# Fetching the shifted rows of v inside SBUF instead of through DRAM, with the middle row read in place

## What is computed

```python
def _dcn(x, ...):
    xproj = x @ inproj_w + inproj_b                      # v: the values that are sampled
    x1 = gelu(layernorm(dwconv3x3(x)))
    offset = x1 @ off_w + off_b
    m = softmax((x1 @ mask_w + mask_b).reshape(B, H, W, G, P), -1)
    out = _dcnv3_core(xproj, offset, m)                  # sampling, 8 groups x 9 points
    return out @ outproj_w + outproj_b

def _dcnv3_core(x, offset, mask):
    xp = pad(x, 1)
    loc = ref + dil_grid + offset / norm                 # 9 points per group and pixel
    # bilinear: 4 neighbours of each point, each weighted, zero outside the padded image
    sampled = gather(y0, x0) * w00 + gather(y0, x1) * w01 + gather(y1, x0) * w10 + gather(y1, x1) * w11
    return (sampled * m).sum(-1)
```

## Time and profile before

| | us |
|---|---|
| median of 3 runs | 101.66 |
| the profiled execution | 101.21 |
| its span (first to last instruction) | 99.3 |
| PE, DVE, ACT, POOL busy | 87.2, 60.1, 45.5, 31.7 |

### The profile page before, as it was taken

How to read it: one execution, slowest core, us unless ns; L and a number is a source line. 1 busy time by engine, 2 the same in 40 slices (tenths; PEclk the granted TensorE clock), 3 DMA queues, 4 the chain that set the end, 5 groups by cost and what they waited for, 6 DMA issues and landing times.

```text
span 99.3 us, 2669 instructions
## 1 busy us (share of the span) xinstructions
PE 87.2 (88%) x1109; PEld 58.3 (59%) x1109; DVE 60.1 (61%) x149; ACT 45.5 (46%) x100; POOL 31.7 (32%) x47
## 2 busy tenths in 40 slices
PE   4989999999978999119999999898999997799980
PEld 1446568558948998013473476574977785564330
DVE  1269673215899929579603416697830969827770
ACT  0470076479887110100003344869535889785000
POOL 7979988500034729779200000000000000400000
PEclk9999999999999999955599999999999999999999
DMA  1996000000448999600000000000000000000003
GB/s 27 367 424 241 23 0 7 0 7 0 160 103 219 219 239 201 139 0 7 3 7 0 0 7 0 0 0 0 0 0 7 0 0 0 0 0 0 0 7 109
DMA packets 1869, 6.26 MB, mean 63 GB/s; under 512 B 288, under 2 KB 800, under 8 KB 1600
## 3 DMA queue, kind: packets, MB, share of 16 engines
q1 hardware_dynamic: 1424, 4.66, 17.9%
q10 hardware_dynamic: 432, 1.42, 3.7%
HBM read 5.16 MB, written 0.92 MB: 61 GB/s over the span
## 4 chain that ended last, share of the span: by engine, by line
PE 56%; DMA 16%; DVE 13%; ACT 6%; SPq 2%; issue 2%; DVEq 0%; ACTq 0%
PE ps L1193 55%; DMA v_win<-v_padded 13%; DMA v_padded<-v_tok 3%; ACT prod L804 2%; SPq L521 2%; DVE prod L984 2%; ACT prod L867 1%; DVE smax L1025 1%; DVE prod L1059 1%; ACT upad L702 1%; DVE res L1188 1%; DVE prod L1063 1%; DVE v_tok L922 1%; DVE ln_room L975 1%; SPq L514 1%
## 5 line engine op out<-in xcount | busy, mean ns | idle before, releaser
L1193 PE MATMUL ps<-terms,wts 64*128 64x256 f32 (+4 forms) x72 | 12.5, 365 | 1.8 <-DVE terms L958 0.9
L1193 PE MATMUL ps<-prod,ident 32*32 32x512 f32 (+1 forms) x216 | 10.3, 755 | 3.7 <-DVE prod L984 3.7
L688 POOL TENSOR_TENSOR terms<-terms 128x256 f32<-128x256 f32 x2 | 1.5, 750 | 36.3 <-DVE terms L1075 36.3
L1193 PEld LDWEIGHTS ps<-terms,wts 128*128 128x128 f32 (+1 forms) x72 | 9.1, 189 | 3.8 <-issue 1.4
L1193 PE MATMUL ps<-prod,wts 128*64 128x256 f32 (+1 forms) x56 | 10.8, 394 | 0.2
L984 DVE TENSOR_TENSOR prod<-v_win,ps 128x1280 f32<-128x1280 f32 x6 | 8.6, 1481 | 3.6 <-DMA v_win<-v_padded 3.6
L603 POOL TENSOR_TENSOR prod<-v_win,a_rows_sb 128x1280 f32<-128x1280 f32 x4 | 9.6, 2413 | 3.1 <-DMA v_win<-v_padded 3.1
L1193 PEld LDWEIGHTS ps<-prod,ident 32*32 32x32 f32 (+1 forms) x216 | 5.2, 118 | 7.6 <-issue 6.4
L1193 PEld LDWEIGHTS ps<-prod,wts 128*64 128x64 f32 (+1 forms) x56 | 6.0, 158 | 3.6 <-DVE prod L1183 1.3
L611 POOL TENSOR_TENSOR terms<-ym,near_hat 128x864 f32<-128x864 f32 x2 | 4.0, 2024 | 12.1 <-DVE ym L950 12.1
L1193 PE MATMUL ps<-idle 128*128 128x512 bf16 x19 | 6.6, 486 | 1.3 <-DVE idle L873 1.3
(11 more groups left out here) (182 smaller groups left out, 172.2 us busy)
## 6 DMA issues: line engine op xcount, KB each, us to landing
v_win<-v_padded SPq DMA_DIRECT2D x4, 640.0 KB, 9.2
wts<-in_w ACTq DMA_DIRECT2D x1, 984.0 KB, 8.1
wts<-in_w SPq DMA_DIRECT2D x1, 640.0 KB, 7.7
v_padded<-v_tok SPq DMA_DIRECT2D x4, 128.0 KB, 3.0
wts<-in_w ACTq DMA_DIRECT2D x1, 280.0 KB, 4.1
x_in<-in_x SPq DMA_DIRECT2D x1, 256.0 KB, 3.2
out<-res SPq DMA_DIRECT2D x2, 128.0 KB, 1.9
wts<-in_w SPq DMA_DIRECT2D x1, 193.0 KB, 3.9
```

Source lines behind the costliest of these rows:

```text
L688: g.tensor_tensor(base_out[:, bl, :], t2[:, bl, :], x2[:, bl, :], ALU.add).then_inc(base_done, 1)
L1193: return nc.tensor.matmul(out_, lhsT, rhs, start=start, stop=stop, skip_group_check=True)
```

## The change

It replaces the way through DRAM by transfers from v_tok to v_win inside SBUF. For dy = 3, 0, 4, 1 and each half of partitions one transfer shifts v_tok by 4 or 8 partitions into the row dy of v_win (60 or 56 partitions of 2 KB), eight per bl, sixteen in all. The edge partitions of each row, for which the window lies outside the image, are cleared ahead by eight small transfers into v_win. The row dy = 2 isn't copied: `window(bl, 2)` reads v_tok itself. VectorE does the rows in the order 2, 0, 1 and waits for v_above[bl] (rows 0 and 1) only at the rows 0 and 1; GpSimd waits for v_below[bl] (rows 3 and 4). TensorE sums in the order 2, 3, 0, 1, 4. The image in DRAM is still stored, behind the row transfers, for the far branch, which now waits for v_stored.

```diff
--- before.py
+++ after.py
@@ -42,7 +42,7 @@
 
 VP = math.isqrt(XQ * VR * VWX - 1) + 1
 
-ROWS = (0, 1, 3, 2, 4)
+ROWS = (2, 3, 0, 1, 4)
 TILE = 32
 TG = P // TILE
 PE5, PE3 = 20, 9
@@ -52,7 +52,11 @@
 
 POOLED = (3, 4)
 
-PRODUCT_ORDER = ((0, 0), (0, 1), (0, 2), (1, 0), (1, 1), (1, 2))
+
+VECTOR_ROWS = (2, 0, 1)
+PRODUCT_ORDER = tuple((bl, dy) for bl in range(BL) for dy in VECTOR_ROWS)
+
+FETCHED = (3, 0, 4, 1)
 
 WARM = {"projection": 8, "conv5": 2, "weights": 3, "close_l0": 2, "route": 4}
 
@@ -129,7 +133,7 @@
         sq, lnv, rstd, xn = (ln_room[:, i * BL:(i + 1) * BL, :] for i in range(4))
         x1 = sb("x1", [P, BL, HW])
         v_tok = sb("v_tok", [P, BL, CELLS])
-        v_win = sb("v_win", [P, BL, K5, VWX * C])
+        v_win = sb("v_win", [P, BL, K5, CELLS])
         past = sb("past", [P, BL, 2 * NPT * XG])
         minus_ident = sb("minus_ident", [P, P])
         lmax = sb("lmax", [P, BL, XG])
@@ -166,7 +170,7 @@
         s_min = sb("s_min", [P, NPT * XG])
         s_v = sb("s_v", [P, W * C])
 
-        zeros = s_v[0:B * XQ, 0:2 * CELLS]
+        zeros = s_v[0:2 * XQ, 0:BL * CELLS]
 
         v_blocks = v_dram.rearrange("b y x c -> b (y x c)")[:, 0:XQ * VR * CELLS].rearrange(
             "b (q r n) -> b q r n", q=XQ, r=VR)
@@ -256,7 +260,7 @@
         x_loaded = sem("x_loaded")
         pads_zero = sem("pads_zero")
         zeros_set = sem("zeros_set")
-        v_cleared = sem("v_cleared")
+        edges_cleared = sem("edges_cleared")
         ones_set = sem("ones_set")
         idle_set = sem("idle_set")
         diag5_set = sem("diag5_set")
@@ -385,13 +389,31 @@
 
         route_step = [sem(f"route_step{bl}") for bl in range(BL)]
         v_stored = [sem(f"v_stored{bl}") for bl in range(BL)]
-        v_windowed = [sem(f"v_windowed{bl}") for bl in range(BL)]
+        v_above = [sem(f"v_above{bl}") for bl in range(BL)]
+        v_below = [sem(f"v_below{bl}") for bl in range(BL)]
         slow_loaded = [sem(f"slow_loaded{bl}") for bl in range(BL)]
 
 
         def grid(ap):
 
             return ap.rearrange("p (y x) -> p y x", y=H)
+
+        def edge_rows(bh, dy):
+
+            p0, p1_ = half(bh)
+            n = abs(dy - K5 // 2) * XQ
+            return (p0, p0 + n) if dy < K5 // 2 else (p1_ - n, p1_)
+
+        def inner_rows(bh, dy):
+
+            p0, p1_ = half(bh)
+            n = abs(dy - K5 // 2) * XQ
+            return (p0 + n, p1_) if dy < K5 // 2 else (p0, p1_ - n)
+
+        def window(bl, dy):
+
+            row = v_tok[:, bl, 0:VW] if dy == K5 // 2 else v_win[:, bl, dy, 0:VW]
+            return bass.AP(row.tensor, row.offset, [list(row.ap[0]), [C, K5], [GC, XG], [1, GC]])
 
         def tokens(tile, bl, bh, xl):
 
@@ -501,25 +523,27 @@
                 sp.dma_start(wts[:, CUTS[i]:CUTS[i + 1]], A_w[:, CUTS[i]:CUTS[i + 1]]).then_inc(w_loaded[i], 16)
 
             sp.wait_ge(zeros_set, 1)
-            for r in (0, VR - 2):
-                for b in range(B):
-                    sp.dma_start(v_blocks[b, :, r:r + 2, :].rearrange("q r n -> q (r n)"),
-                                 zeros[b * XQ:(b + 1) * XQ, :]).then_inc(v_cleared, 16)
-            sp.wait_ge(v_cleared, 2 * B * 16)
+            for dy in FETCHED:
+                for bh in range(BH):
+                    e0, e1 = edge_rows(bh, dy)
+                    sp.dma_start(v_win[e0:e1, :, dy, :], zeros[0:e1 - e0, :].rearrange("p (b n) -> p b n", b=BL)
+                                 ).then_inc(edges_cleared, 16)
+            sp.wait_ge(edges_cleared, len(FETCHED) * BH * 16)
             for bl in range(BL):
                 sp.wait_ge(v_copied, bl + 1)
+                for dy in FETCHED:
+                    for bh in range(BH):
+                        d0, d1_ = inner_rows(bh, dy)
+                        s0 = d0 + (dy - K5 // 2) * XQ
+                        sp.dma_start(v_win[d0:d1_, bl, dy, :], v_tok[s0:s0 + d1_ - d0, bl, :]).then_inc(
+                            (v_above if dy < K5 // 2 else v_below)[bl], 16)
+            for bl in range(BL):
                 for bh in range(BH):
                     p0, p1_ = half(bh)
                     inside = v_blocks[BL * bh + bl, :, 2:2 + H, :].rearrange("q y n -> y q n")
                     sp.dma_start(inside, v_tok[p0:p1_, bl, :]).then_inc(v_stored[bl], 16)
             for bl in range(BL):
                 sp.wait_ge(v_stored[bl], 16 * BH)
-                for bh in range(BH):
-                    p0, p1_ = half(bh)
-                    rows = bass.AP(v_dram.tensor, v_blocks[BL * bh + bl, 0, 0].offset,
-                                   [[CELLS, H], [VR * CELLS, XQ], [1, K5 * CELLS]])
-                    sp.dma_start(v_win[p0:p1_, bl, :, :].rearrange("p y n -> p (y n)"),
-                                 rows).then_inc(v_windowed[bl], 16)
             for bl in range(BL):
                 sp.wait_ge(res_done, bl + 1)
                 sp.dma_start(out[:, bl * HW:(bl + 1) * HW], res[:, bl, :]).then_inc(out_stored, 16)
@@ -595,10 +619,9 @@
 
             def products(bl, dy):
 
-                pool.wait_ge(v_windowed[bl], 16 * BH)
+                pool.wait_ge(v_below[bl], 16 * BH * len(POOLED))
                 pool.wait_ge(a5_copied, bl + 1)
-                row = v_win[:, bl, dy, 0:VW]
-                win = bass.AP(row.tensor, row.offset, [list(row.ap[0]), [C, K5], [GC, XG], [1, GC]])
+                win = window(bl, dy)
                 weights = a5_rows_sb[:, bl, dy - AR, :].rearrange("p (d x) -> p d x", d=K5)
                 g.tensor_tensor(prod[:, bl, dy, :, :].rearrange("p d (x c) -> p d x c", c=GC), win,
                                 weights.unsqueeze(3).broadcast_to([P, K5, XG, GC]),
@@ -623,6 +646,7 @@
                 with pool.If(is_far > 0):
 
                     pool.wait_ge(samp_done, bl + 1)
+                    pool.wait_ge(v_stored[bl], 16 * BH)
 
                     pos = s_pos[:, bl, :, :].rearrange("p c n -> p (c n)")
                     for axis in range(2):
@@ -976,11 +1000,12 @@
 
             def products(bl, dy):
 
-                if dy == 0:
-                    dve.wait_ge(v_windowed[bl], 16 * BH)
+                if dy == K5 // 2:
+                    dve.wait_ge(v_copied, bl + 1)
                     dve.wait_ge(a5_done, bl + 1)
-                row = v_win[:, bl, dy, 0:VW]
-                win = bass.AP(row.tensor, row.offset, [list(row.ap[0]), [C, K5], [GC, XG], [1, GC]])
+                else:
+                    dve.wait_ge(v_above[bl], 16 * BH * (K5 // 2))
+                win = window(bl, dy)
                 v.tensor_tensor(prod[:, bl, dy, :, :].rearrange("p d (x c) -> p d x c", c=GC), win,
                                 a5_rows(bl, dy, dy + 1)[:, 0].unsqueeze(3).broadcast_to([P, K5, XG, GC]),
                                 ALU.mult).then_inc(prod_done, 1)
@@ -1084,9 +1109,9 @@
             far_terms(1, 0)
             far_terms(1, 2)
             for bl in range(BL):
-                for dy in range(K5 - len(POOLED)):
+                for dy in VECTOR_ROWS:
                     products(bl, dy)
-                    if bl and dy == 1:
+                    if bl and dy == VECTOR_ROWS[0]:
                         flags(0)
                         flags(1)
             mask_sums(0)
```

## The result

The changed kernel takes 96.56 us (median of 4 runs, 96.16 to 96.85), the kernel before beside it 101.69 us. The ratio is 0.952, 95% interval 0.946 to 0.957. On another chip, with more runs, it was 0.943 (0.938 to 0.948). The prediction was 96.3, with a range of 95.2 to 98.5.

A forecast was written before the change was run, and what follows sets the result against it. It took the v passage through DRAM, mostly volume, and the slab sum's halved clock as the bound. An earlier start (2.9 us) and full clock (2.2) gave 5.1 us: 96.1 from the profile, 96.6 from the median, stated 96.3, range 95.2 to 98.5.

The forecast's parts named there:

- The floor: Start of half 1's products: gate moves from the 42.73 set by DRAM to about 39.80, set by a5_done(1).
- The slab sum: TensorE's window sum: starts 41.43, takes 7.1 us at full clock, ends 48.5 instead of 53.61; gain 5.1 us.
- B: Rival: TensorE's clock falls all the same, slab sum keeps 9.25 us; gain 2.9, 98.3 us; chance 0.10.
- GpSimd: GpSimd's products of rows 3 and 4: half 1's end at 42.76 and 45.15, neither later than TensorE.
- The transfers: 16 SBUF-to-SBUF transfers on SP's queue: 0.64 us an issue, some 4 us of margin everywhere, cost 0.
- The landing: Time from a row transfer's issue to its landing: taken as 3.3 us, from a span of 1.9 to 3.3.
- the 38 that was to show it right: Sign for the row transfers into v_win: all 16 landed before 38 us.
- Rival C: SBUF-to-SBUF transfers move at half rate, 108 GB/s, 1.1 us each; gain 3.7, 97.5 us; chance 0.08.
- Rival D: Row transfers become the wait: at 1.24 us each, 102.9 us; decides from 1.13 us a transfer; chance 0.03.
- Rival E: Each row transfer pays its landing before the next begins: 16 take 30.4 us, time 110.3 us; chance 0.01.
- The clears: Eight edge clears, now into SBUF: at 4.6 to 7.1 us as before, with time until 24 us.
- VectorE: VectorE's six products as before: 1.48 us each, 1.43 apart, three in 4.28 us.

The follow-up runs named there:

- e1: The kernel before, with 14 dummy matmuls put into TensorE's wait ahead of the slab sum; ratio 0.964 (0.957 to 0.970).
- e3: The kernel before, five rows still loaded from DRAM, middle row multiplied in place and first, sum order 2, 3, 0, 1, 4; ratio 0.962, 98.3 to 98.6 us.
- e6: The kernel after, each of the 16 transfers cut in two by columns, 32 issues of the same total bytes; ratio 1.058, 106.9 us.
- e2: The kernel after, with the middle row also copied into v_win, 20 transfers instead of 16; ratio 0.950, 96.8 to 97.8 us.
- e7: The kernel after, with the transfers of both bl merged into 8 of 224 or 240 KB; 96.66 us in one execution.
- e12: The kernel before with middle row in place and first, four rows from DRAM in 8 loads, on one chip with after; ratio 0.941, 95.6 to 96.4 us.
- e9: The kernel before, unchanged, traced a second time; its slab sum took 9.41 us, no whole time given.

## Why the prediction was right

- **The floor.** a5_done(1) at 39.78 as the next gate: VectorE's fourth product began at 39.91, with the wait for TensorE in front of it (predicted 39.80).
- **The slab sum.** Start 41.55 (41.43), length 6.87 (7.1), end 48.42 (48.5). The gain of 5.1 us came as 5.2, split 2.8 and 2.4 where I had 2.9 and 2.2. That the clock would hold over gaps of 0.6 and 0.8 us was right (B fell); e1 shows its share by itself, and e3 that it holds over 1.68 us too. One argument for it was misread: the gaps were called a fifth of "the 3.66 us after which it fell", but the clock fell 1.8 us into that idle (40.70 to about 42.5; its share is 0.73 from 42 to 43), and 1.3 us into another in e6. The margin was smaller than the prediction took it to be.
- **GpSimd.** Its row 4 was done at 45.2, as worked out, and never gated the sum. The far branch was again not entered.
- **The transfers.** Here a term was mis-sized: 0.64 us an issue, taken from the stores, is 0.83 from start to start. The nearest row of before was of 64 partitions; in e2 such transfers take 0.58 and those of 60 and 56 partitions 0.77 beside each other. They differ in more than the number of partitions: the 64 are moved without a shift. The landing was sized too long: from the start of the last issue the sum had 3.9 us (0.64 and 3.3), and e2 shows 3.0. The last rows landed near 39.6 instead of 37.6, past the 38 that was to show it right, and the room at the tightest gate was 1.9 us instead of 3.7. The cost was 0 as predicted because the slack was larger than the error, not because the term was right; e2, with four transfers more, is past the edge.
- **Rival C** (half rate, 108 GB/s) fell: after moved 139 to 160 GB/s while its issue bound it, and e7 212 and 218. **Rival D** was the right danger: its point of decision, 1.13 us a transfer, lies 0.3 above what was measured, and e6 at 1.63 a row is 5.8% slower. **Rival E**, the fixed part of a small transfer paid in series, fell: e2's transfers of 128 KB landed 2.3 us (median) after their issue, 16 of that in series would take 37 us, and the sixteen were through in about 15.5.
- **The clears** cost 0.68 us an issue instead of 0.32, until 10.5, and had until 24.
- **VectorE.** Three products in 4.28 us, each 1.48 long, start 1.40 apart, not 1.43; nothing hangs on it.
- **What I had not seen**: the prediction called most of the way through DRAM volume, but took the whole passage to be what has to go. The volume of the fifth row made the data late: with four rows the same path is as fast (e12). The prediction's number did not depend on it, but its picture of what the change removes did.

## What to carry to other kernels

When a chain of transfers ends late, first ask which part of the data the consumer already has, and let it start there: with the order of rows to suit, that gave 3.8% here (e3), and it kept the clock. Count issues as well as bytes: 16 transfers of 116 KB were bound by 0.83 us each on one queue, and 32 of half the size turned a gain of 5% into a loss of 6%. A wait of TensorE can cost twice, once as the wait and once as the slow work behind it (2.4 us behind a wait of 3.7, nothing behind one of 1.68), so a shortened wait can be worth more than its length.

## What the runs showed of the hardware

- The issue of a transfer SBUF to SBUF took 0.58 us for 64 partitions of 2 KB and 0.77 for 60 or 56 of them, in the same execution (e2; the 64 unshifted, the others shifted by 4 or 8 partitions), and 0.78 whether 2 KB or 1 KB went per partition (e6). With twice 2 KB per partition it was 0.85 (e7).
- The small clears took 0.32 us each into DRAM as 4 x 1024 elements and 0.68 into SBUF as 4 or 8 x 2 x 512.
- A transfer of 128 KB from v_tok to v_win landed 2.3 us (median) after its issue; VectorE started on the last one of 120 KB 3.0 us after its issue began (e2), on one of 60 KB 2.3 us after (e6).
- The granted clock held at 1.00 over an idle TensorE of 0.8 us (after) and 1.68 us (e3); it fell to 0.50 during idles of 2.27, 3.66 and 3.77 us (e6, before, e9), and that 1.3, 1.8 and 2.2 us after they began. So the length of the idle alone doesn't say whether it falls: e3 went past the 1.3 of e6. It came back 4.9 and 5.2 us after the slab sum began (before, e9). In e6 40 records in 3.9 us did not bring it back.
